# A decoder layer on one core: order of the last routing steps, layout of the experts' results, place of the mask loads, two splits moved into the block loop

## What is computed

```python
x = x + delta_rule_attention_and_mlp(layernorm(x))            # stage 1
x = x + cross_attention(layernorm(x), ctx, ctx, mask)         # stage 2: 16 heads of 16
xt = layernorm(x)                                             # stage 3
probs = sigmoid(xt @ gate_w.T + gate_b)                       # 6 experts
w, idx = top_k(probs, 2);  w = w / (w.sum(-1) + 1e-8)
ge = (one_hot(idx, 6) * w[..., None]).sum(1)
for e in range(6):
    y += ge[:, e:e+1] * ((silu(xt @ ew1[e].T) * (xt @ ew3[e].T)) @ ew2[e].T)
z = (silu(xt @ fc1.T) * (xt @ fc2.T)) @ fc3.T                 # shared expert
x = x + y + z
```

## Time and profile before

| | us |
|---|---|
| median of three runs (lowest, highest) | 1457.79 (1456.06, 1459.02) |
| the profiled execution, its own time | 1457.25 |
| its span | 1455.4 |
| stage 1 and the turn to stage 2, until about | 545 |
| steps of stage 2, until about | 1149 |
| drain with the shared groups 0 to 3 | 1149 to 1211 |
| 61 blocks | 1211 to 1391 |
| tail | 1391 to 1455 |

### The profile page before, as it was taken

One profiled execution on the slowest core, in us unless ns is written; L12 is line 12 of the kernel. 1 busy time (PEld: TensorE's weight loads), 2 busy tenths in 40 slices (PEclk: granted clock), 3 DMA queues, 4 the chain that ended last, 5 costly groups with the idle time before them and its releaser, 6 DMA issues. The chain is left out here.

```text
span 1455.4 us, 34511 instructions
## 1 busy us (share of the span) xinstructions
PE 1300.1 (89%) x11121; PEld 1171.7 (81%) x11121; DVE 906.3 (62%) x2926; ACT 654.5 (45%) x1526; POOL 522.8 (36%) x716
## 2 busy tenths in 40 slices
PE   5999999999987599999999999999999876888976
PEld 4888988988987578888888888888888775777865
DVE  4676476576564466777666777667767474444546
ACT  3543433433423144555555555555555643444531
POOL 3233133133124313433444334443343651233344
PEclk9999999999988888999999999999999988999987
DMA  8699200000002264656556565566653332222367
GB/s 188 140 232 244 69 0 0 0 0 0 0 21 61 52 158 105 134 134 132 119 118 137 132 141 120 114 131 132 142 139 92 86 109 66 81 85 86 102 163 194
DMA packets 134974, 151.39 MB, mean 104 GB/s; under 512 B 41235, under 2 KB 118404, under 8 KB 134868
## 3 DMA queue, kind: packets, MB, share of 16 engines
q1 hardware_dynamic: 128148, 134.55, 40.1%
q0 software_dynamic: 6160, 15.69, 3.4%
q10 hardware_dynamic: 576, 0.07, 0.0%
HBM read 79.27 MB, written 45.82 MB: 86 GB/s over the span
## 5 line engine op out<-in xcount | busy, mean ns | idle before, releaser
L2142 DVE CUSTOM_DVE_ANT_0 junk<-psum,biasq 112x375 f32<-112x375 f32 x512 | 270.8, 542 | 152.4 <-issue 104.6
L1624 ACT ACTIVATE pr<-psum 125x448 f32<-125x448 f32 x384 | 205.5, 545 | 93.0 <-PE psum L1126 87.9
L1126 PE MATMUL psum<-qst,kst 97*125 97x224 f32 x768 | 226.6, 356 | 0.0
L1106 PE MATMUL psum<-kst,qst 96*112 96x376 f32 x512 | 187.9, 381 | 27.1 <-DMA qst<-qlo 19.4
L1126 PEld LDWEIGHTS psum<-qst,kst 97*125 97x125 f32 x768 | 147.9, 193 | 7.2 <-issue 0.2
L1121 PE MATMUL psum<-flagk,negbig 125*125 125x448 bf16 x384 | 140.0, 364 | 0.0
L1106 PEld LDWEIGHTS psum<-kst,qst 96*112 96x112 f32 x512 | 89.5, 180 | 56.7 <-DVE smax L2142 28.0
L700 POOL TENSOR_TENSOR rs<-rs,neg_half 112x1 f32<-112x1 f32 x32 | 18.2, 570 | 322.0 <-DVE rs L2055 319.9
L829 POOL DMA_INDIRECT routed_y<-yb,yrow x61 | 59.1, 968 | 138.5 <-ACT yb L1795 132.8
L1140 PE MATMUL psum<-pr,vaug 125*32 125x112 f32 x3072 | 95.1, 265 | 0.0
L1140 PEld LDWEIGHTS psum<-pr,vaug 125*32 125x32 f32 x3072 | 71.4, 111 | 15.9 <-issue 11.4
(11 more groups left out here) (306 smaller groups left out, 3544.0 us busy)
## 6 DMA issues: line engine op xcount, KB each, us to landing
kst<-khi SPq DMA_DIRECT2D x64, 376.0 KB, 6.8
routed_h<-in_route_pad SPq DMA_DIRECT2D x6, 3640.0 KB
kst<-klo SPq DMA_DIRECT2D x32, 376.0 KB, 9.5
ctxT<-in_ctxT SPq DMA_DIRECT2D x32, 375.0 KB, 6.2
hblk<-routed_h SPq DMA_DIRECT2D x61, 130.0 KB, 2.1
qst<-qhi SPq DMA_DIRECT2D x128, 56.0 KB, 4.5
stage<-in_e SPq DMA_DIRECT2D x21, 256.0 KB, 3.2
maskq<-in_mask SPq DMA_DIRECT2D x32, 164.1 KB
```

What stands on the lines that cost most here:

```text
L1106: pe.matmul(bank[max_bank(n, hd)][0:T, 0:S2E], head(qst[par][0:ROWS], hd), pair(kst[par][0:ROWS], hd // 2), start=True, stop=True).then_in ...
L1126: mm = pe.matmul(bank[q % 3][0:KP, cols(i, 2 * T)], pair(kst[par], n)[:, cols(q // HPB, KP)], both(qst[par], n), start=False, stop=True, s ...
L1624: nc.scalar.activation(pr[q % PROBS][:].rearrange("k i q -> k (i q)"), bank[q % 3][0:KP, 0:GT], ACT.Exp, scale=1.0 / HD ** 0.5).then_inc(s ...
L2142: nc.vector.tensor_tensor_reduce(out=junk[:, hd % 2, :], in0=bank[max_bank(n, hd)][0:T, 0:S2], in1=biasq[:, par, :], scale=1.0, scalar=-3e ...
```

## The change

Four edits, with names as above.

1. SP's `load_masks` is moved from behind `store_turned` to the end of the step, behind `spread_max`.
2. The drain's lists on PE, ACT, DVE and POOL are reordered, the routing of rows 30 and 31 earlier among the shared groups. `low_shared` of groups 0 to 5 goes from POOL to DVE. `totals` no longer waits for `count_choice(B)` (removed): it adds `chosen` of the last row with a second small matmul. `plan_blocks` counts on the semaphore `slot` and stands before `add_shared(1)`.
3. Groups 4 and 5: SP's `load_turned(4)` and `(5)` move behind the load of block 3, ACT's `high_shared` into blocks 5 and 6, DVE's `low_shared` into blocks 6 and 7. SP reads 4 starts first, then 16 each at i = 4, 20, 36 and the last 9 at i = 52.
4. Token numbers are doubled, a first choice adds 1, not CAP: a token's two results are neighbouring rows of `ybuf`. `load_products` issues one DMA per group with rows of 2 KB into one tile.

```diff
             def step(t, par, load=True, heads=True):          # SP
...
                 if load:
-                    load_masks(*ahead(t, par, 3))
                     load_context(*ahead(t, par, 3))
                 if heads:
                     spread_heads(*ahead(t, par, 2))
                 spread_max(*ahead(t, par, 1))
+                if load:
+                    load_masks(*ahead(t, par, 3))
...
-            load_turned(4)
-            load_turned(5)
...
-                for r in range(TOP):
-                    src = ybuf[r * CAP + g * GT:r * CAP + (g + 1) * GT, :].rearrange("(j t) d -> t j d", j=GB)
-                    sp.dma_start(products[r][g % RINGS], src).then_inc(s3[f"first_in{g % RINGS}"], 16)
+                src = ybuf[TOP * g * GT:TOP * (g + 1) * GT, :].rearrange("(j t r) d -> t j (r d)", j=GB, r=TOP)
+                sp.dma_start(products[g % RINGS].rearrange("t j r d -> t j (r d)"), src).then_inc(s3[f"first_in{g % RINGS}"], 16)
...
             for i in range(NBLK):
-                if i % OWNERS == 0:
-                    starts = starts_of(i)
-                load_block(i, starts[i % OWNERS])
+                if i == 0:
+                    starts = list(starts_of(0, RINGS))
+                elif i % OWNERS == RINGS:
+                    starts += starts_of(i, OWNERS)
+                load_block(i, starts[i])
+                if i == RINGS - 1:
+                    load_turned(4)
+                    load_turned(5)
...
             step(ROUNDS + 1, 0, masks=False, power=False)     # POOL
-            low_shared(0)
-            low_shared(1)
...
+            decide(*ahead(ROUNDS + 1, 1, -1))
             rsqrt3(ROUNDS + 1, 1)
-            decide(*ahead(ROUNDS + 1, 1, -1))
...
-            count_choice(B)
-            low_shared(4)
-            low_shared(5)
...
             def totals():                                     # PE
-                pe.wait_ge(s3["gating"], DECIDED * B + 1)
-                pe.wait_ge(s3["slot"], 3 * B)
-                pe.matmul(bank[2][0:P, 0:NE], earlier[:, T:T + P], counted[:], start=True, stop=True).then_inc(s3["place_ps"], 1)
+                pe.wait_ge(s3["gating"], DECIDED * (B - 1) + 7)
+                pe.matmul(bank[2][0:P, 0:NE], earlier[0:T, T:T + P], chosen[:], start=True, stop=False)
+                pe.matmul(bank[2][0:P, 0:NE], earlier[:, T:T + P], counted[:], start=False, stop=True).then_inc(s3["place_ps"], 1)
...
+            place(*ahead(ROUNDS + 1, 1, -2))
             transpose_row(*ahead(ROUNDS + 1, 1, -1))
             half_shared(0, 0, 0)
             transpose_o(ROUNDS + 1, 1)
+            route(*ahead(ROUNDS + 1, 1, -1))
...
             half_shared(0, 1, 1)
-            route(*ahead(ROUNDS + 1, 1, -1))
+            place(*ahead(ROUNDS + 1, 1, -1))
             half_shared(1, 0, 0)
+            transpose_row(ROUNDS + 1, 1)
             half_shared(1, 0, 1)
-            transpose_row(ROUNDS + 1, 1)
+            route(ROUNDS + 1, 1)
             half_shared(1, 1, 0)
             half_shared(1, 1, 1)
-            place(*ahead(ROUNDS + 1, 1, -1))
             contract_shared(0)
-            route(ROUNDS + 1, 1)
-            expand_shared(2)
+            half_shared(2, 0, 0)
+            place(ROUNDS + 1, 1)
+            totals()
...
             for i in range(NBLK):                             # ACT
                 silu_block(i)
+                if i in (5, 6):
+                    high_shared(i - 1)
...
+            low_shared(0)                                     # DVE
+            low_shared(1)
+            slots(*ahead(ROUNDS + 1, 1, -2))
+            add_gate_bias(*ahead(ROUNDS + 1, 1, -1))
             normalise_heads(ROUNDS + 1, 1)
+            choose(*ahead(ROUNDS + 1, 1, -1))
...
+            add_gate_bias(ROUNDS + 1, 1)
+            low_experts(1)
+            choose(ROUNDS + 1, 1)
             shared(1)
-            slots(*ahead(ROUNDS + 1, 1, -1))
             add_shared(0)
-            add_gate_bias(ROUNDS + 1, 1)
             low_experts(2)
-            choose(ROUNDS + 1, 1)
-            shared(2)
+            slots(ROUNDS + 1, 1)
+            low_experts(1)
+            low_shared(3)
+            hidden(2, 0)
+            low_hidden(2, 0)
+            hidden(2, 1)
+            low_hidden(2, 1)
+            plan_blocks()
             add_shared(1)
             low_experts(3)
             shared(3)
-            slots(ROUNDS + 1, 1)
             low_experts(2)
             add_shared(2)
-            low_experts(2)
-            plan_blocks()
             add_shared(3)
...
             for i in range(NBLK):
                 hidden_block(i)
                 output_rows(i)
+                if i in (6, 7):
+                    low_shared(i - 2)
```

More of the change, by code:

```diff
@@ L115, in shape_constants @@
     before[:, 0:T] = np.arange(T + 1)[:, None] < col
-    tokens = ((np.arange(RB)[None, :] - RB) * T + row).astype(np.float32)
+    tokens = (TOP * ((np.arange(RB)[None, :] - RB) * T + row)).astype(np.float32)
     pad = np.zeros((NE + SPARE, BLK, ROW), np.float32)
@@ L286, in decoder_layer @@
             e13 += [w3("e13_lo", [P, NE, DC, 2, EW], F32R)]
-            products = [[e13[r][:].bitcast(F32).rearrange("p e c w n -> p (e c w n)")[0:T, n * GB * D:(n + 1) * GB * D].rearrange("t (j d) -> t j d", j=GB)
-                         for n in range(RINGS)] for r in range(TOP)]
+            products = [e13[n // 2][:].bitcast(F32).rearrange("p e c w n -> p (e c w n)")[0:T, n % 2 * GB * TOP * D:(n % 2 + 1) * GB * TOP * D].rearrange("t (j r d) -> t j r d", j=GB, r=TOP)
+                        for n in range(RINGS)]
         apart = {nc.gpsimd.engine: sem("pool_waited"), nc.vector.engine: sem("dve_waited")}
@@ L718, in decide @@
                 count_choice(b)
[L719 removed]
+                nc.gpsimd.tensor_scalar(told(par, C_TOKEN), told(par, C_TOKEN), float(TOP * RB * T), None, ALU.add).then_inc(s3["gating"], 1)
                 wait_apart(pool, s3["prob"], SORTING * (b + 1))
@@ L832, in add_products @@
                 n = g % RINGS
-                pool.wait_ge(s3[f"first_in{n}"], 16 * TOP * (g // RINGS + 1))
-                nc.gpsimd.tensor_tensor(products[0][n], products[0][n], products[1][n], op=ALU.add).then_inc(s3["both"], 1)
+                pool.wait_ge(s3[f"first_in{n}"], 16 * (g // RINGS + 1))
+                nc.gpsimd.tensor_tensor(products[n][:, :, 0], products[n][:, :, 0], products[n][:, :, 1], op=ALU.add).then_inc(s3["both"], 1)
             for i in range(NBLK):
@@ L1424, in _ @@
             transpose_o(ROUNDS + 1, 1)
+            route(*ahead(ROUNDS + 1, 1, -1))
             half_shared(0, 0, 1)
             transpose_on(ROUNDS + 1, 1)
-            place(*ahead(ROUNDS + 1, 1, -2))
             half_shared(0, 1, 0)
@@ L1750, in _ @@
             high_experts(1)
+            exponential_gate(*ahead(ROUNDS + 1, 1, -1))
             copy_on(ROUNDS + 1, 1)
-            shared(0)
-            exponential_gate(*ahead(ROUNDS + 1, 1, -1))
+            silu(0, 0)
+            high_hidden(0, 0)
+            silu(0, 1)
+            high_hidden(0, 1)
+            high_experts(2)
             keep_h(ROUNDS + 1, 1)
             high_shared(2)
-            high_experts(2)
+            exponential_gate(ROUNDS + 1, 1)
+            high_experts(1)
             shared(1)
-            high_experts(2)
+            high_experts(3)
             high_shared(3)
-            exponential_gate(ROUNDS + 1, 1)
             shared(2)
@@ L2273, in add_routed @@
                 dve.wait_ge(s3["x_new"], added("routed", g) - 1)
-                nc.vector.tensor_tensor(x[:, group(g), :], x[:, group(g), :], products[0][g % RINGS], op=ALU.add).then_inc(s3["x_new"], 1)
+                nc.vector.tensor_tensor(x[:, group(g), :], x[:, group(g), :], products[g % RINGS][:, :, 0], op=ALU.add).then_inc(s3["x_new"], 1)
             e13_pieces = iter(range(3 + NE, 3 * (NE + 1)))
@@ L2314, in plan_blocks @@
                 step_done(11)
-                nc.vector.scalar_tensor_tensor(out=start_i[:].unsqueeze(2), in0=owner[:], scalar=float(CAP // BLK), in1=start[:].unsqueeze(2), op0=ALU.mult, op1=ALU.add).then_inc(s3["gating"], 1)
+                nc.vector.scalar_tensor_tensor(out=start_i[:].unsqueeze(2), in0=owner[:], scalar=float(CAP // BLK), in1=start[:].unsqueeze(2), op0=ALU.mult, op1=ALU.add).then_inc(s3["slot"], 1)
+            low_shared(0)
+            low_shared(1)
+            slots(*ahead(ROUNDS + 1, 1, -2))
@@ L2317, in _ @@
+            add_gate_bias(*ahead(ROUNDS + 1, 1, -1))
             normalise_heads(ROUNDS + 1, 1)
+            choose(*ahead(ROUNDS + 1, 1, -1))
             low_experts(1)
-            slots(*ahead(ROUNDS + 1, 1, -2))
             add_row(ROUNDS + 1, 1)
@@ L2328, in _ @@
             low_hidden(0, 1)
-            add_gate_bias(*ahead(ROUNDS + 1, 1, -1))
-            choose(*ahead(ROUNDS + 1, 1, -1))
+            slots(*ahead(ROUNDS + 1, 1, -1))
             low_experts(2)
+            low_shared(2)
+            add_gate_bias(ROUNDS + 1, 1)
```

(8 more changed lines are left out.)

55 lines of the change are left out of this document (26 added, 29 removed).

## The result

The changed kernel takes 1438.64 us (median of 4 runs, 1435.44 to 1440.19), the kernel before beside it 1456.92 (4 runs); the ratio is 0.9872 with a 95% interval of 0.9849 to 0.9895, or 18.7 us less (15.3 to 22.0). The prediction was 1433.3: direction and range hold, and the time is 5.3 us above it. The profiled execution is the slowest of the four (1440.19, span 1438.1).

A forecast was written before the change was run, and what follows sets the result against it. PE, busy 89% of the span, bounds the kernel; its 155 us idle and low-clock stretches can be won. Terms -17 - 6.5 - 0.5 - 0.5 = -24.5 from 1457.25 give 1432.8, median 1433.3 us; range 1422 to 1445.

The forecast's parts named there:

- Part 1: Loop of stage 2: with masks issued last, the wait for the last q copy into `qst` goes, -17 us.
- the step of 19.43 us: Late loop step loading neither masks nor context, taken as model for 26 steps averaging 20.12 us: a gain of 17.9.
- rival A: Loop: another wait replaces the one at the step's opening, half of the 17 given back, 1442 us; chance 0.14.
- both bounds, -10 and -20: Loop term's edges: -10 if waits leave a rest, -20 with all of 17.9 and two openings before 560.
- Part 2: Drain: reordered lists and `low_shared` on DVE bring the first block's transposition from 1211.17 to 1204.7, -6.5 us.
- Rival B: Drain gains nothing: PE waits for `place` of row 30 and DVE, cold clock lasts longer; 1439.8 us; chance 0.12.
- the predicted wait for `place(30)`: Drain: the new order makes PE wait about 2.7 us for `place` of row 30.
- Rival E: Drain: POOL's expert splits hold up DVE's `low_shared`, +2.5 us at most, 1435.8; counted within the forecast's 0.62.
- Part 3: Blocks: three remaining SP reads, the last of 9 rather than 13, shorten PE's waits, -0.5 us (0 to -1).
- I cost them at nothing: Blocks: two DVE subtractions of 1.2 us each fall in idle time, cost nothing; 2.4 us if uncovered.
- Part 4: Tail: product loads with half the DMAs and 2 KB rows for 1 KB, same bytes, -0.5 us.
- bounds of -3 and +1.5: Tail: -3 us if product loads reach 296 GB/s, +1.5 if strided `ybuf` writes cost what reads save.

The follow-up runs named there:

- e5: The changed kernel again, no line different, on the second chip: 1420.88 us, ratio 0.9725 to the kernel before.
- e7: Changed kernel with both row scatters behind the mask bias and the splits of groups 4 and 5 in blocks 14 and 15: 1418.52 us, ratio 0.9709.
- e8: As e7, with a token's two results in two regions again (1 KB rows, eight loads): 1417.10 us, ratio 0.9703.
- e10: Changed kernel with both row scatters of a step behind the mask bias, on the third chip: 1419.98 us, ratio 0.9726.
- e1: Kernel before with only the masks' loads moved to the end of SP's step: 1449.82 us against 1460.19, ratio 0.9932.
- e6: Changed kernel with the masks' loads in front again in SP's step, on the second chip: 1450.91 us, ratio 0.9926.
- e12: Kernel before with both row scatters of a step behind the mask bias, on a fourth chip: 1431.33 us against 1461.94, ratio 0.9787.
- e3: Changed kernel with the two splits of groups 4 and 5 in blocks 14 and 15 instead of 6 and 7: 1436.94 us, ratio 0.9845.
- e9: The changed kernel a third time, unaltered, on the third chip: 1437.61 us, ratio 0.9844.

## Why the prediction was right, and where it was off

**Part 1, -17, was -11.9 in the trace of after and is the term with the wrong mechanism behind its size.** Right: the wait for `qst` goes, the copies land in 1.9 us, SP's new queue harms nobody. Over the 26 steps of the prediction's sum the gain is 12.2 us where it had 17.9. It was wrong in two ways. First, the step of 19.43 us that I took as the model was not a step without waits. Its timeline, from 1094.32 on:

```profile
1101.35 0.94 POOL L742 DMA_INDIRECT routed_h<-h,slot  x1 [0.30 <-issue]
1102.90 0.53 ACT L1629 COPY pv<-psum 128x448 f32<-128x448 f32 x1 [2.37 <-remote]
...
1103.74 0.43 PE L1106 MATMUL psum<-kst,qst 96*112 96x376 f32 x1 [0.20 <-DVE smax L2142]
```

The copy is at 8.58, held, and PE waits for a row maximum. So I read a floor of 19.43 where e5, e7, e8 and e10 show 18.97. Second, the hold, visible in before as the copy's place 1.5 to 1.8 us behind the second scatter in all but one of 25 steps, was not looked for, since PE hardly waited for it: 2.7 us in 8 waits. That is rival A in kind; its price was half of the 17, and what e1 shows is 9.9 us of gain in place of 17. Against it I had cited the 19.43 us step, which could not speak against it. Where nothing is held the term is -30 (e5 against e6), outside both bounds, -10 and -20. They were built from listed waits, and e6 lists 20.7 us of waits for `qst` where its steps lose 29.7 against e5's.

**Part 2, -6.5, was -11.0**, and ten further traces with this drain agree (69.7 to 70.2 against 81.1 to 82.8). The order was followed rightly; to compare, I add 11.9 to after's times. `choose(31)` ends at 1167.8 (predicted 1168.5); the plan starts at 1179.4 (1181.3), since DVE's work ahead of it took 11.6 us and not 12.8; the queue of DVE behind the plan is 9.1 us (10.0). So `contract_shared(3)` starts at 1192.6 (1195.3), which is 2.7 of the 4.5 us that the term was short. It fills 4.6 us at a granted clock of 0.63, the lower level for most of it (5.0): 0.4. The read of the experts then costs 2.93 us and not 4.43: 1.5. In after's own time its first instruction ran at 1182.1, 3 us before PE's matmuls of the contraction ended, so the start of the read lay beside them; in the blocks, from which I took 4.43, little lies ahead of it. The mis-sized terms are thus DVE's work ahead of the plan and behind it, and the read. Rival B was out: the predicted wait for `place(30)` came (2.25, predicted 2.7), and the drain gained all the same. Rival E's kind appeared, at an instruction I hadn't named: a cast of two columns took 3.62 us beside three expert splits of POOL of 3.73, where the loop's cast takes 0.19. The Trainium skill's page SBUF — State Buffer (section SBUF: two separate sides) has a GpSimd operation and a DVE operation in a mode that uses two ports exclude each other for the whole instruction. By that rule, the trace agrees, but it doesn't show in which mode this cast ran.

**Part 3, -0.5, was a loss.** The gain from SP's reads did not come: PE waits 1.41, 1.39 and 1.13 us behind them, before 1.48, 1.47 and 1.02. And "I cost them at nothing", said of the splits, is the failing step. The six traces without splits in blocks 6 and 7 have blocks of 185.7 us on average (184.9 to 187.2), the eight with them 187.6 (185.7 to 189.5): +1.9. Up to the scatter of block 20 the two sets don't overlap: 68.9 to 70.0 us against 70.7 to 72.0. The medians don't show the loss. What was delayed was indeed wanted later by PE's matmuls, as I had reasoned, but PE's own queue stands at that wait with its read behind it. The split in block 7 makes `hblo` 1.0 us later; the read starts at 1213.0, 0.4 us after the matmuls of `contract_block(6)` began, in before at 1235.2, 0.6 us ahead of them. The read itself lasts some 5.7 us in both; what differs is how much of it lies beside PE's matmuls (before, then after; duration in ns, then the start):

```profile
L1258 PEldq TENSOR_LOAD <-owner_i x1: 1118/1118/1118, 1235.2 to 1235.2; - x1
...
L1254 PEldq TENSOR_LOAD <-owner_i x1: 1292/1292/1292, 1213.0 to 1213.0; - x1
```

The gap is 5.5 to 5.6 us in all eight and 4.4 in all six, and in after the clock is at its lower level behind it (an operation of 1.22 us, 0.72 in the earlier trace rows). I had named 2.4 us as the price if uncovered and had looked for the cover at PE's matmuls, not at its reads.

**Part 4, -0.5, can't be told from nothing.** The tail was 58.5 to 62.0 us in nine traces with 2 KB rows (mean 59.7) and 58.7 to 60.1 in five with 1 KB rows (59.4); e7 and e8 differ by 1.4 us in their medians. The 2.9 us that the tail of after lost lie within the spread of 3.5 between traces with the same rows and can't be put down to the change. The prediction's bounds of -3 and +1.5 hold.

**Luck.** The time came near the forecast because 4.5 us too little in the drain's term offset 5 us too much in the loop's; the blocks and the tail of that one execution make up the 5 to 7 us that are left. The same kernel on the second chip took 1420.9 us, 40 less than before: there the range of 1422 to 1445 (-35 to -13) fails, on the term of the loop. The range's slow end is also tighter than the bounds that it names: -10 - 1 + 1.5 and half of 2.4 make -8.3, not -13, and nothing in the prediction says why.

## What to carry to other kernels

When a wait is to be removed, look in the trace for events that are late without anybody waiting for them; they are what will be waited for next. Don't take a floor from a step of the same kernel unless PE's busy time in it is the least of all steps: small stalls count as busy (19.34, 19.23 and 18.98 us for the same 209 or 210 operations, in before, after and e5). When an operation is put ahead of another because "it is wanted later", ask what the waiting engine has queued behind that wait, register reads above all; and when a queue is congested, look for who lets its first member go, since moving two instructions on the releasing engine (e12, 31 us) was worth as much as reordering the queue where nothing is held (30 us, e5 against e6), and three times as much as reordering it where the hold stays (e1, 9.9 us, on another chip than e12).

## What the runs showed of the hardware

- Two instructions on two engines, ACT's copy and DVE's fifth maximum, start 1.5 to 1.9 us behind the start of GpSimd's last indirect DMA ahead of them, though PE's work for them is over up to 2 us before. It was so in before and after, on one chip in e1 to e3, on another in e9; on a third (e5, e6) it was absent, though e5 is the same program as after and e9. Two scatters in front hold them to 8.7 to 9.3, one to 7.3, none to 6.95. In e10, with the scatters at 8.5 to 9.9, every operation of ACT and DVE stands within 0.1 us of its place in e5. By what way the scatter does this, and what sets the one chip apart, stays open. That it is an accident of a single load of a program is unlikely but not excluded: with both scatters in front, three kernels of three show it on the first chip and none of two on the second.
- The same product loads ran at 202 to 259 GB/s over the 15 us that begin some 10 us behind the last scatter (after 206, e5 202, e3 259).
- PE's read of 16 registers lasts 5.6 to 6.1 us (after, before). The first one in the blocks leaves 4.4 us of idle PE, 5.5 us if it starts 1 us later, and the one ahead of the blocks 2.2 to 3.2 us behind a contraction (the eleven traces with the new drain), during which its first instruction is already under way.
